# Layer 2 of a gated four-layer decoder: norm, router, scores, mixing weights and basis network as one pipeline over tiles

## The reference

```python
probs = jax.nn.softmax(xt @ w_router, axis=-1)
topk_p, topk_idx = jax.lax.top_k(probs, TOPK)
topk_w = topk_p / (jnp.sum(topk_p, axis=-1, keepdims=True) + EPS)
gate = (xt @ w_gate).reshape(T, K, I)
up = (xt @ w_up).reshape(T, K, I)
basis = jax.nn.silu(gate) * up
p = amplitudes[..., 0] ** 2 + amplitudes[..., 1] ** 2
mix = p / (jnp.sum(p, axis=-1, keepdims=True) + EPS)
mixed = jnp.einsum('tek,tki->tei', mix[topk_idx], basis)
down = jnp.einsum('tei,ih->teh', mixed, w_down)
out = jnp.einsum('teh,te->th', down, topk_w * expert_scale[topk_idx])
out = out + jax.nn.silu(xt @ shared_w_gate) * (xt @ shared_w_up) @ shared_w_down
```

## Time and profile before

| what | us |
| --- | --- |
| median of 3 runs | 4015.32 |
| the profiled execution, its own time | 4010.64 |
| the span of its profile | 4008.6 |
| TensorE busy (matmul) in the span | 2881.3 (72%) |
| VectorE busy in the span | 2286.4 (57%) |
| ScalarE busy in the span | 1469.7 (37%) |
| GpSimd busy in the span | 868.9 (22%) |

### The profile page before, as it was taken

One profiled execution on the slowest core, in us unless ns is written; L12 is line 12 of the kernel. 1 busy time (PEld: TensorE's weight loads), 2 busy tenths in 40 slices (PEclk: granted clock), 3 DMA queues, 4 the chain that ended last, 5 costly groups with the idle time before them and its releaser, 6 DMA issues. The chain is left out here.

```text
span 4008.6 us, 60740 instructions
## 1 busy us (share of the span) xinstructions
PE 2881.3 (72%) x19894; PEld 1816.7 (45%) x19894; DVE 2286.4 (57%) x4602; ACT 1469.7 (37%) x2927; POOL 868.9 (22%) x1207
## 2 busy tenths in 40 slices
PE   5388864565999955797166973688869716999993
PEld 5133324222555533233133752344447615888883
DVE  7699975575777766334686977555569630000003
ACT  5277751352222244797143541111135301112110
POOL 3011111573333354111001320000023142111110
PEclk7599995897999975899587986899989758999997
DMA  7766611996222244882001421100024121121113
GB/s 252 169 120 120 120 52 38 350 356 255 81 80 80 81 133 127 137 119 33 23 0 59 139 73 42 40 10 10 12 98 138 33 101 45 58 67 51 55 53 127
DMA packets 270503, 394.33 MB, mean 98 GB/s; under 512 B 57345, under 2 KB 197870, under 8 KB 269984
## 3 DMA queue, kind: packets, MB, share of 16 engines
q1 hardware_dynamic: 243408, 321.15, 30.0%
q0 software_dynamic: 25152, 68.22, 4.9%
q10 hardware_dynamic: 1680, 1.57, 0.2%
HBM read 231.94 MB, written 164.44 MB: 99 GB/s over the span
## 5 line engine op out<-in xcount | busy, mean ns | idle before, releaser
L2581 POOL DMA_INDIRECT rows_out<-e_out,e_tr_dest x224 | 234.5, 1047 | 870.7 <-DVE e_out L3204 508.8
L1183 ACT ACTIVATE a_pt<-a_psS 128x512 f32<-128x512 f32 x512 | 277.5, 595 | 155.4 <-PE a_psS L1081 151.0
L3204 DVE COPY e_out<-e_psD 128x512 f32<-128x512 f32 x40 | 27.6, 691 | 491.9 <-PE e_psD L3172 491.7
L1205 DVE TENSOR_REDUCE a_mx_sb<-a_psM 128x4 f32<-128x1024 f32 x256 | 292.9, 1213 | 18.9 <-PE a_psM L1064 17.7
L2972 PE MATMUL e_psG<-e_wgu,e_yT 128*128 x576 | 275.0, 600 | 25.7 <-ACT e_yT L3000 23.1
L1095 PE MATMUL a_psV<-a_pt,a_vt 128*18 128x256 f32 x4096 | 292.0, 387 | 1.2 <-issue 0.8
L3172 PE MATMUL e_psD<-e_w,e_hT 128*128 128x256 f32 x1280 | 289.7, 386 | 0.0
L3161 PE MATMUL e_psH<-e_yT,e_w 128*128 128x256 f32 x1280 | 284.5, 381 | 1.6 <-issue 0.8
L3104 ACT ACTIVATE e_hT<-e_psH 128x512 f32<-128x512 f32 x160 | 95.5, 597 | 452.0 <-PE e_psH L3161 452.0
L3172 PEld LDWEIGHTS e_psD<-e_w,e_hT 128*128 128x128 f32 x1280 | 245.5, 194 | 33.1
L3161 PEld LDWEIGHTS e_psH<-e_yT,e_w 128*128 128x128 f32 x1280 | 244.1, 191 | 35.5 <-issue 2.1
(11 more groups left out here) (376 smaller groups left out, 5908.9 us busy)
## 6 DMA issues: line engine op xcount, KB each, us to landing
kbd<-e_bgu SPq DMA_DIRECT2D x64, 512.0 KB, 5.0
cr_kbd<-kbd SPq DMA_DIRECT2D x64, 512.0 KB, 3.4
rows_in<-zeros POOLq DMA_DIRECT2D x36, 522.0 KB, 6.3
e_xin<-rows_in SPq DMA_DIRECT2D x144, 128.0 KB
vbd<-e_bd SPq DMA_DIRECT2D x64, 272.0 KB, 3.7
cr_vbd<-vbd SPq DMA_DIRECT2D x64, 272.0 KB, 2.7
cq_rows<-rows_out SPq DMA_DIRECT2D x32, 512.0 KB, 5.8
e_w<-in_L_ffn_w_dram SPq DMA_DIRECT2D x16, 1024.0 KB, 7.8
```

Of the source, the lines that this page charges most:

```text
L1183: act.activation(pt[:, probs(t, h), b, :, :], psS[:, unit(t, h, b) % S_BANKS, :].rearrange("p (k c) -> p k c", k=KC), ACT.Exp, scale=scale ...
L1205: dve.tensor_reduce(mx[:, t % 2, :, h, :], psM[:, k % 2, :, :].rearrange("p b (f c) -> p b f c", f=2), AX_X, ALU.max).then_inc(ring_read, 1)
L2581: pool.indirect_dma_start(out=self.rows_out[0:limit, :], out_offset=bass.IndirectOffsetOnAxis(ap=self.dest[:, t:t + 1], axis=0), in_=rows, ...
```

## The change

The five stages become one. `basis_weights` allocates the weights ahead of the attention stage of layer 2, and its `prefetch` issues their six loads from SyncE's list of that stage, behind the keys of tile 8. The new `phase_basis_ffn` loads only the router's weights, the amplitudes and the scales. In iteration s of an unrolled loop it works on tile s of the basis network, s+1 of the router and the scores, s+2 of the turning, s+3 of the normed rows and s+4 of the statistics. The turned rows stay in SBUF (three buffers), so DRAM is not used between. The 4096-wide instructions for the scores become instructions on 128 numbers for each tile; the sums of exponentials come from the activation itself (`accum_out`). The blend's 1024 products and its reduction become two half sums (`half_m`) that eight instructions on 128 numbers fill in turn, and one addition. In the turned rows' PSUM bank the right half takes the turned normed rows, the left half the output. The core of the diff:

```diff
+                    if t == 8 and prefetch is not None:
+                        prefetch(sp)
...
+                def turn_rows(t):
+                    pe.wait_ge(y_ready, t + 1)
+                    if t >= 4:
+                        pe.wait_ge(added, t - 3)
...
+                def route(t):
+                    pe.wait_ge(y_copied, t + 1)
+                    if t >= 1:
+                        pe.wait_ge(lg_ready, t)
+                    if t >= 2:
+                        pe.wait_ge(small_copied, t - 1)
+                        pe.wait_ge(c_ready, t - 1)
...
+                for s in range(-2, TILES + 1):
+                    if ok(s + 1):
+                        route(s + 1)
+                    if ok(s):
+                        gates(s)
+                        turn_scores(s)
+                    if ok(s + 2):
+                        turn_rows(s + 2)
+                    if ok(s - 1):
+                        turn_mixed(s - 1)
+                    if ok(s):
+                        share(s)
+                        coefficients(s)
+                        ups(s)
+                    if ok(s - 1):
+                        downs(s - 1)
...
+                def blend(t):
+                    v = t % 2
+                    dve.wait_ge(c_done, t + 1)
+                    dve.tensor_copy(cf[:, v, :], psC[:, C_MIX]).then_inc(c_ready, 1)
...
+                for s in range(TILES + 1):
+                    if ok(s):
+                        gelu_gate(s)
+                        shared_rows(s)
+                    if ok(s + 1):
+                        choose(s + 1)
+                    if ok(s + 4):
+                        statistics(s + 4)
+                    if ok(s + 3):
+                        normed_rows(s + 3)
+                    if ok(s + 1):
+                        score(s + 1)
+                    if ok(s):
+                        blend(s)
+                    if ok(s - 1):
+                        residual(s - 1)
...
-        phase_norms(core, "n5")
         with ExitStack() as c:
-            score = core.sb(c, "score2", [P, TILES, 128], F32)
-            mix = core.sb(c, "mix", [P, 8], F32)
-            with ExitStack() as c2:
-                logits = core.sb(c2, "logits2", [P, TILES, 128], F32)
-                phase_project(core, "l2", 128, logits, weight_cols=a["L2_ffn_w_router"], yT_all=yT)
-                phase_topk(core, "t2", 128, 4, logits, score, 1.0, "eps")
-            phase_mix(core, "mx", a["L2_ffn_amplitudes"], a["L2_ffn_expert_scale"], mix)
```

More of the change, by code:

```diff
@@ L1498, in vector_end, with phase_cross @@
             self.lay(dve, i)
-def phase_cross(core, name, kbd_dram, vbd_dram, wq, bq, gq, wo, bo, gate):
+def phase_cross(core, name, kbd_dram, vbd_dram, wq, bq, gq, wo, bo, gate, prefetch=None):
     nc = core.nc
@@ L2167, in phase_basis_ffn, with ok, column @@
         psC = ps(ctx, n + "psC", [P, 512])
+        C_SCORE, C_LOGIT, C_MIX = slice(0, E), slice(E, 2 * E), slice(2 * E, 2 * E + K)
+        def ok(t):
+            return 0 <= t < TILES
+        def column(tile, t):
+            return tile[:, t:t + 1]
         with nc.Block() as block:
@@ new lines, in turn_mixed, with share @@
+                def turn_mixed(t):
+                    pe.wait_ge(shared, t + 1)
+                    pe.wait_ge(mixed, t + 1)
+                    if t >= 1:
+                        pe.wait_ge(m_copied, t)
+                    for k in range(3):
+                        ins = pe.transpose(psT[:, k * P:(k + 1) * P], m[:, t % 2, k, :], core.ident[:, :])
+                    ins.then_inc(m_turned, 1)
+                def share(t):
+                    if t >= 1:
+                        pe.wait_ge(shared, t)
+                    for k in range(KC):
+                        ins = pe.matmul(psS[:, :], yT[:, t % 3, k, :], ws[:, k, :, :], start=(k == 0), stop=(k == KC - 1))
+                    ins.then_inc(s_done, 1)
@@ new lines, in coefficients, with ups @@
+                def coefficients(t):
+                    if t == 0:
+                        pe.wait_ge(mix_ready, 1)
+                    pe.wait_ge(small_copied, t + 1)
+                    pe.matmul(psC[:, C_MIX], scT[:, t % 2, :], mix[:, :], start=True, stop=True).then_inc(c_done, 1)
+                def ups(t):
+                    if t >= 1:
+                        pe.wait_ge(basised, t)
+                    for c in range(2):
+                        for k in range(KC):
+                            ins = pe.matmul(psU[:, c, :], yT[:, t % 3, k, :], wu[:, k, c * 512:(c + 1) * 512], start=(k == 0), stop=(k == KC - 1))
+                    ins.then_inc(u_done, 1)
@@ new lines, in residual @@
+                def residual(t):
+                    dve.wait_ge(down_done, t + 1)
+                    dve.scalar_tensor_tensor(out=core.xs[:, t, :], in0=psO[:, 0:DIM], scalar=gate, in1=core.xs[:, t, :],
+                                             op0=ALU.mult, op1=ALU.add).then_inc(added, 1)
+                for t in range(2):
+                    statistics(t)
+                normed_rows(0)
+                for t in range(2, 4):
+                    statistics(t)
+                normed_rows(1)
```

344 lines of the change are left out of this document (218 added, 126 removed).

## The result

The changed kernel takes 3858.92 us, the median of 3 runs (3858.22 to 3869.85), against 4015.32: a ratio of 0.962, 95% interval 0.9605 to 0.9638. The forecast was 3856, in a range of 3828 to 3892. The profiled execution took 3858.92 us as well, with a span of 3857.2 (before 4010.64 and 4008.6).

What follows compares the result with a forecast made beforehand. The prediction took TensorE, with a gap waiting for VectorE's blend, to bound the middle, after a head with TensorE mostly idle. Savings of 147.2 + 7 + 5 = 159 us gave 3851.5, plus 4.7 for the median: 3856 us, range 3828 to 3892.

Steps and rivals of the forecast that it cites:

- The head: Stretch up to the stage's first turned scores: 11.9 us forecast against 159.1 before, 147.2 us less.
- The middle: The 31 periods from first to last turned scores: 372 us forecast, 12.0 each, against 379.0, 7 us less.
- The ring: Loop from VectorE's shared rows through copied coefficients, router, gates and turned rows back to shared rows: 12.0 us a tile.
- four picks of 128, 3 x 0.20 + 0.31: VectorE's picks between shared rows and copied coefficients, priced at a 0.20 us pace: 0.91 us a tile.
- The second ring: Next loop of hand-overs, over the residual and `turn_rows`: 11.6 us a tile, claimed not to bind.
- The covers: ScalarE's exponentials lie beside places, statistics and normed rows: 1.2 us cover for 0.9; uncovered, 0.3 us a tile.
- tail: Stretch after the last turned scores: 14.1 us forecast against 19.1, 5 us less.
- TensorE bound: Rival: the coefficient hand-over comes in time, 11.3 us a tile, 22 us less, 3834 us; chance 0.15.
- Full durations: Rival: about ten small VectorE instructions cost duration, not pace; 12.8 us a tile, 3881 to 3893 us; chance 0.25.
- Attention hurt: Rival: first gates wait for loads or attention keys come late, +5 to +15 us, 3861 to 3871; chance 0.05.
- the change doesn't do what it says: Rival: tiles run without lookahead in the head, 12.4 us a tile after it, 3868 us; chance 0.04.
- Slower: Rival: TensorE and VectorE take turns through `route`; break-even at a 10.1 us list, wholly in turn 4138 us; chance 0.03.

Runs made afterwards that it cites:

- one_pointer: Changed kernel with picks multiplying by the constant 0.25 instead of the row's weight, leaving softmax weights out of the scores; 3848.25 us, ratio 0.9582.
- copy_early: Changed kernel with VectorE's copy of the coefficients moved from the blend to right behind the shared rows; 3856.44 us, ratio 0.9604.
- ring_open: Changed kernel with the next tile's top four, statistics and normed rows moved ahead of the gate on VectorE's list; 3832.81 us, ratio 0.9554.

## Why the prediction was right

**The head** was right as a sum (11.1 for 11.9) and in its reason: norms, router, top four and scores left the path. That the sum came so close is in part luck, since two of its parts were off in opposite directions. From the landed router's weights to the first gates it took 2389.11 - 2384.84 = 4.3 us for a forecast 3.5: between the two router products stand the turned rows of tile 1 and the wait for their copy, 1.1 us together, where the sum had 0.4. The gates took 4.0 for 5.8. Their granted clock was 0.86 behind 4.3 us of turnings and router products, and 0.60 before behind 95 us without a matmul. Over all runs the head came out between 11.0 and 12.0 with the loads early, and the gates' clock is most of that spread.

**The middle** was right in mechanism: the wait sits at L2257, released by L2449, with nothing at L2282. The ring was mis-sized by 0.3 us a tile, and the period is 11.45 us of TensorE's work and 0.86 of wait for the forecast's 11.3 and 0.7. Link by link, from the steady tile: shared rows 0.80 (forecast 0.79), top four 0.85 (0.85), statistics 0.55 (0.51), normed rows 0.32 (0.33), denominator to weights 0.65 (0.63), **four picks 1.15 (0.91)**, additions 0.74 (0.72), **coefficients and hand-over 0.30 (0.20)**, router 0.52 (0.6), gates 3.43 (3.44), turned scores and rows 0.32 (0.31), turned mixed rows to shared rows 2.67 (2.72). The sum is 12.30; measured 12.31. The step that failed is "four picks of 128, 3 x 0.20 + 0.31": I gave an instruction with two pointer operands the pace of MAX8. With one pointer it has that pace, and the period is 12.07. Some luck lies in the sum of the middle: 31 periods of 12.31 would be 381.6, and the four short ones at the ends, which the prediction did not have, gave 2.9 back. So of the 7.4 us by which the profiled execution missed 3851.5 the middle is 6.7, head and tail cancel (-0.8 and +0.8), and 0.7 lies outside the stage. In one_pointer, whose picks have the pace that was taken, the middle is 371.4 us for the 372 forecast; there the 0.07 us a tile of the other links and the short ends cancel.

**The second ring** was put at 11.6 us and measures 12.18 where it binds, in copy_early. VectorE's list up to the scores is 5.06 there for 4.74 (the picks are 0.24 of it), the blend with the copied coefficients 3.62 for 3.5, and the residual with its hand-over 0.58 for 0.4. It does not bind in the changed kernel, so the miss cost the forecast nothing; but it would have misled whoever opened the first ring only. "TensorE's own work 11.3" measures 11.21 where nothing else binds.

**The covers** held. The exponentials take 0.77 us after their start (2544.79 to 2545.56) and were hidden beside places, statistics and normed rows; the last tiles, without those two, show the bare wait:

```profile
2754.45 0.16 DVE L2409 SCALAR_TENSOR_TENSOR bs_den<-bs_den 128x1 f32<-128x1 f32 x1 [0.36 <-ACT bs_ex_sb L2349]
```

That is the uncovered 0.3 of the prediction. GpSimd's column held nothing in the steady tile: the denominator follows the normed rows 0.32 us after their start and lasts 0.15. The **tail**, 14.9 for 14.1, is a sum of three misses: 6.6 us to the end of the ups for 5.7 (0.4 of it a wait at L2282 for the blend of the tile before, which the steady tiles don't have), 3.75 for the last blend where 3.5 was taken, and 4.55 for the rest where 4.9 was taken. The median came out 3 us from the forecast and not 7 by luck: the profiled execution of the changed kernel lies at its median where that of before lay 4.7 under it.

**The rivals.** *TensorE bound* was false for this change, and true for ring_open: 11.21 us a tile, and 3833 and 3826 us, where 3834 was worked out for it. *Full durations* is refuted: the statistics, aggregates, MAX8 and places kept their paces, and 12.8 a tile did not come. The picks, though, made a third of that step real. *Attention hurt* and *the change doesn't do what it says* left no trace. *Slower* was far off: the list is 5.06 us, not 10.1.

On the Trainium skill's page "VectorE: DVE Perf Modes" (The DRAIN you can't avoid), by which the next instruction does not start until the pipe is empty: the prediction left out the end of that paragraph, by which a next instruction that is not held starts earlier. Held, by the section that it points to (Two Vector instructions with no wait between them), is one that starts only when every earlier VectorE instruction has finished. Taken as full durations, four picks would last 4 x 0.343 = 1.37 us and the six additions 6 x 0.347 = 2.08. The runs show 1.11 and 1.66, so each instruction that follows freely starts 0.08 to 0.09 us before the end of the one ahead, and the measurement decides for paces.

## What to carry to other kernels

In a pipeline over tiles, look for the rings: from an engine's wait, follow the releaser's own list back to what started it. Work of other tiles that stands in the list between a late input and the value another engine waits for lies wholly on the tile, however idle the engine is elsewhere. Put it ahead of the next wait instead, and leave enough work to cover a copy's or an exponential's latency; here that alone gave 33 us. Then find the second ring before opening the first: it lay 0.13 us behind. Price a small instruction by the row of its own form (operands and pointers), not by one of the same size, and count the shorter periods at both ends of the pipeline apart from the steady ones.

## What the runs showed of the hardware

- On VectorE, 128 fp32 numbers a partition cost 282 ns with one pointer operand and 343 ns with two; one pointer and two tensors take 347 ns, two tensors without a pointer 289. Groups of VectorE instructions of the changed kernel (busy us, mean ns):

```profile
L2460 DVE SCALAR_TENSOR_TENSOR bs_half_m<-bs_b,bs_cf,bs_half_m 128x128 f32<-128x128 f32 x192 | 53.1, 347 | 0.0
L2421 DVE TENSOR_TENSOR bs_hot<-bs_hot 128x128 f32<-128x128 f32 x64 | 15.8, 289 | 1.1
L2457 DVE TENSOR_SCALAR bs_half_m<-bs_b,bs_cf 128x128 f32<-128x128 f32 x64 | 15.4, 284 | 1.1
```

- In a row of them the pace from start to start is 0.08 to 0.09 us under the duration: (1.66 - 0.347) / 5 = 0.263 us for the 347 ns form (six in 1.66 us at 2550.27 of the steady tile), (1.11 - 0.343) / 3 = 0.256 for the picks, 0.20 for those with one pointer. Busy time over count, as 53.1 / 192 = 0.277, is more, since the last of a row counts in full. An addition that uses the last pick's result starts 0.04 us after its end (2546.66 + 1.11 to 2547.81).
- Here a value handed from VectorE to TensorE costs 0.30 us from the start of the copy to the start of the product (2548.55 to 2548.85), 0.14 of it after the copy's end.
- Each of ScalarE's exponentials with a sum brings a read of the accumulator of 0.19 us behind it, half of the 0.40 of the exponential of 128 numbers. It starts 0.09 us before the exponential's end, and what it adds to the time was not tested:

```profile
2544.79 0.40 ACT L2348 ACTIVATE bs_exall<-bs_lg_sb,bs_neg 128x128 f32<-128x128 f32 x1 [1.33 <-DVE bs_neg L2401]
2545.10 0.19 ACT L2348 ACTIVATION_READ_ACCUMULATOR bs_exall<-bs_lg_sb,bs_neg 128x1 f32 x1
```

- The first gates of the stage (8 passes) are set by the granted clock, and that differs from run to run: 3.8 to 4.9 us at 0.90 to 0.71 in ten profiles in which TensorE went straight on from router products, 5.3 us at 0.66 in the one in which it had been idle for 5.5 us, 5.8 at 0.60 before, behind 95 us without a matmul, and 3.43 at 1.00 in the steady tiles. 3.43 divided by the granted clock gives each of these within 0.1 us. One run with the idle time does not size what it costs in clock.
